# The last group of a latent-attention layer, its steps behind the attention in two halves of rows

## The chip, the cores and the metric

The kernel runs on one core of one Trainium2 chip. The core's engines are TensorE (PE in the views; PEld is its weight load), VectorE (DVE), ScalarE (ACT), GpSimd (POOL) and SyncE (SP, here only issuing DMAs). The metric is device time of one execution in microseconds (us); lower is better.

## The reference, cut to what matters

A two-layer pre-norm decoder on 4096 rows (16 sequences of 256) of width 256, all float32. The change touches only how the second layer's two attention parts end:

```python
x = x + _L1_attn_ref(_layernorm(x), ...)        # latent attention, 8 heads, latent rank 64
x = x + _L1_xattn_ref(_layernorm(x), ctx, ...)  # one head over 77 context rows, masked, bias
x = x + _L1_ffn_ref(_layernorm(x), ...)         # quantised feed-forward, 256 -> 768 -> 256

def _L1_ffn_ref(x, w_gate, w_up, w_down):
    def act_qdq(x):
        scale = max(max(abs(x)) / (2**15 - 1), 1e-12)   # one scale for the whole tensor
        return clip(round(x / scale), ...) * scale
    x = act_qdq(x)
    ...
```

The scale of `act_qdq` needs the largest magnitude over all 4096 normalised rows. So the feed-forward can't begin before the last row has gone through both attention parts and the last layer norm.

## The kernel before, in words

The program is written by hand, engine by engine, with semaphores; each engine runs its own list in order. Stages follow each other in blocks: layer 0, experts, `layer1` (latent attention and context attention, L1408 on), `feed_forward`. Each block ends with a barrier of all engines.

`layer1` works on eight groups of 512 rows (two sequences; four tiles of 128 rows, `NT` = 4, `NG` = 8). The attention itself runs in slots: `t` counts them, eight to a group (`NS` = 8: two sequences times four pairs of heads), so group `g` has slots 8g to 8g+7. In slot `t` TensorE does `scores(t)`, then `turn(t - 1)` (transposes of the probabilities), then `values(t - 2)`. DVE does the maxima, `by_key` (copies one half of the turned probabilities) and `invert`; ACT does `exponents(t)`, `heads(t - 2)` (copy of the head outputs) and its own `by_key(t - 1)`; POOL divides the probabilities by their sum. Around these stand, at fixed places of a slot, the other steps of the groups, with a group's tail running one to three groups late:

- `project(g, b)` (L1849): output projection of half `b` (256 rows) of a group, then `add_heads(g, b)` on DVE into `x4`.
- `moments(1, g)` (DVE: four BN_STATS, four BN_AGGR, the variance), `deviation` (POOL: a power of -0.5, L1725), `shifts` (DVE), `normalise` (ACT, four tiles, L1983), `turn_norm` (PE, eight transposes, L1825) and two copies of the banks to `hT` (ACT, L1949).
- `x_scores` (PE, L1866), `masked` (DVE, three operations, L2107 to L2114), `x_exponents` (ACT, L1988), `x_turn` (PE, L1874), a copy to `xPT` (ACT), `x_values` (PE, L1883, one bank for each 256 rows), `add_context` (DVE, L2127) into `x5`.
- `moments(2, g)`, `deviation`, `shifts`, `normalise`, `turn_norm`, the copies into `hT_all`, and `largest` (DVE, L2133) into `amax_all`. SyncE stores `x5` to DRAM.

For the last group (number 7, slots 56 to 63) nothing of a later group is left to run beside this tail. The loops run to slot `LAST` with the same placing: its `project(7, 1)` comes in slot 66, `turn_norm(1, 7)` in slot 69, and so on. Group 6's `x_turn`, `x_values`, `add_context`, `moments(2)` to `turn_norm(2)` lie in slots 64 to 68, between group 7's.

PSUM banks 5, 6 and 7 serve all these steps in turn: the table `UNITS` gives the order in which steps take a bank, and a step waits (`room`) until the contents of the step three places before it in that order have been read out.

```python
        for t in range(FIRST, LAST):
            g, s = group_step(t)
            for name, ahead, n in UNITS[s]:
                if there(g + ahead):
                    k = turn_of % 3
```

`feed_forward` begins with the largest magnitude: a transpose (L2317), a maximum, a spread (L2322), scale and its inverse, then the first 512 rows are quantised (L2465, L2467) and the matmuls with the gate weights start (L2309), without a gap from there on. Its last pass is the projection down (L2354).

## Time and profile before

| what | us |
| --- | --- |
| median of 3 runs (1717.52 to 1718.95) | 1718.71 |
| the profiled execution's own time | 1720.9 |
| its span, first to last instruction | 1719.2 |
| PE busy in the span | 1539.6 (90%) |
| DVE busy | 976.8 (57%) |
| ACT busy | 847.2 (49%) |
| POOL busy | 465.5 (27%) |
| last slot of attention starts (scores of slot 63 on PE) | 1348.78 |
| last copy of `layer1` ends (ACT) | 1396.55 |
| first gate matmul of `feed_forward` | 1402.10 |
| first matmul of the projection down | 1630.92 |

A busy share is an average over all stages. In the stretch that the change touches, PE is busy 13.94 of 24.50 us and every other engine less. In the chain and the timelines below, a time is us from the span's start; a wait stands in brackets behind an instruction, with the one that ended it. "x16" counts records: a float32 matmul leaves two, a transpose one.

### The profile page before, as it was taken

Reading aid. Unit: us, or ns where it says so; the run is one execution under the profiler, and the core shown is the slowest. Engines: PE = TensorE matmul, PEld = TensorE weight load, DVE = VectorE, ACT = ScalarE, POOL = GpSimd, SP = SyncE. Lnnn points to the kernel's source line nnn. Section 1 sums busy time; section 2 is a strip of 40 time slices with the busy share of each in tenths; the row PEclk is TensorE's granted clock in tenths of the full one; section 3 lists DMA queues with packets and bytes.
Section 4 is the critical chain, followed back from the end, with each engine's and each line's share of the span. In section 5 each row is a group of like instructions: output and inputs, shape, how many; then the busy total and the mean of one; then the engine's idle time right before and its main releaser. Section 6 shows DMA issues by size and latency. Waiting matters only on the chain. (4 is left out here: it accounts for less than half of the span.)

```text
span 1719.2 us, 26943 instructions
## 1 busy us (share of the span) xinstructions
PE 1539.6 (90%) x10059; PEld 1073.2 (62%) x10059; DVE 976.8 (57%) x2262; ACT 847.2 (49%) x1849; POOL 465.5 (27%) x582
## 2 busy tenths in 40 slices
PE   6999999998987889999998999999999869995099
PEld 4677776766665667777787566666666534442088
DVE  3665767766756335222222567667665535599883
ACT  4455564654465322211211565666665523596980
POOL 3222233243334310000002565554533200042000
PEclk9999999998999989999998999999999969998599
DMA  3440111111151143433425211101100000000022
GB/s 112 153 152 16 46 29 44 31 43 42 44 150 41 56 139 123 148 116 117 157 81 139 62 38 50 47 29 31 32 14 13 13 13 0 1 0 13 25 88 72
DMA packets 100912, 108.30 MB, mean 63 GB/s; under 512 B 25394, under 2 KB 89788, under 8 KB 100784
## 3 DMA queue, kind: packets, MB, share of 16 engines
q1 hardware_dynamic: 94640, 90.01, 16.7%
q0 software_dynamic: 6144, 16.57, 3.0%
q8 instruction: 82, 1.34, 0.3%
q14 instruction: 46, 0.38, 0.1%
HBM read 64.77 MB, written 42.01 MB: 62 GB/s over the span
## 5 line engine op out<-in xcount | busy, mean ns | idle before, releaser
L1740 POOL TENSOR_SCALAR c_pr<-c_pr,c_rsum 128x256 f32<-128x256 f32 x256 | 127.5, 515 | 189.4 <-DVE c_rsum L2046 188.7
L1961 ACT ACTIVATE c_pr<-bank,c_nmax 128x256 f32<-128x256 f32 x256 | 118.0, 473 | 119.2 <-DVE c_nmax L2041 111.8
L1511 ACT ACTIVATE b_G<-bank 128x320 f32<-128x320 f32 x128 | 56.0, 437 | 210.2 <-PE bank L1461 210.2
L1461 PE MATMUL bank<-b_XT,shared 128*128 128x320 f32 x512 | 154.0, 435 | 0.0
L2041 DVE TENSOR_REDUCE c_nmax<-bank 128x2 f32<-128x512 f32 x128 | 82.4, 685 | 106.0 <-PE bank L1791 102.9
L1475 PE MATMUL bank<-shared,b_G 128*128 128x256 f32 x640 | 142.2, 379 | 0.0
L1475 PEld LDWEIGHTS bank<-shared,b_G 128*128 128x128 f32 x640 | 120.9, 190 | 17.8
L1060 DVE TENSOR_TENSOR hT_all<-bank,a_causal 128x512 f32<-128x512 f32 x128 | 79.4, 682 | 65.9 <-PE bank L557 65.9
L492 POOL TENSOR_TENSOR a_L<-a_L,a_Lm 128x1232 f32<-128x1232 f32 x32 | 72.0, 2249 | 164.6 <-DVE a_Lm L1075 164.6
L1461 PEld LDWEIGHTS bank<-b_XT,shared 128*128 128x128 f32 x512 | 92.1, 192 | 27.3 <-issue 0.8
L1530 DVE COPY b_Y<-bank 128x256 f32<-128x256 f32 x80 | 33.9, 424 | 120.3 <-PE bank L1475 120.1
L1522 DVE COPY b_XT<-bank 128x256 f32<-128x256 f32 x80 | 34.0, 424 | 100.2 <-PE bank L1448 100.2
L2354 PE MATMUL bank<-wdT,d_raw 128*128 128x256 f32 x384 | 85.0, 385 | 2.5 <-DVE d_raw L2566 2.5
L2309 PE MATMUL bank<-hT_all,wgT 128*128 128x512 f32 x192 | 84.6, 604 | 2.0 <-DVE hT_all L2467 2.0
L1708 POOL MEMSET c_minus<- 128x4 f32 x1 | 0.1, 102 | 312.3 <-POOLq L54 312.3
L1802 PE MATMUL bank<-ident,c_pr 128*128 128x128 f32 x512 | 72.3, 281 | 12.2 <-POOL c_pr L1740 9.0
L2309 PE MATMUL bank<-hT_all,wuT 128*128 128x512 f32 x192 | 82.9, 593 | 0.0
L2354 PEld LDWEIGHTS bank<-wdT,d_raw 128*128 128x128 f32 x384 | 74.3, 194 | 12.9 <-DVE d_raw L2566 2.5
L1072 DVE TENSOR_TENSOR a_L<-bank,a_amask 128x308 f32<-128x308 f32 x128 | 52.2, 470 | 47.3 <-PE bank L572 30.2
L1802 PEld LDWEIGHTS bank<-ident,c_pr 128*128 128x128 f32 x512 | 55.0, 141 | 37.4 <-POOL c_pr L1740 24.7
L1791 PE MATMUL bank<-c_latT,c_qT 64*128 64x256 f32 x512 | 76.8, 407 | 0.6 <-ACT c_pr L1961 0.2
L507 POOL DMA_INDIRECT t_slots_in<-a_h,a_slot_s x64 | 63.2, 987 | 33.1 <-issue 17.1
(346 smaller groups left out, 3399.8 us busy)
## 6 DMA issues: line engine op xcount, KB each, us to landing
shared<-L_ffn_w SPq DMA_DIRECT2D x32, 512.0 KB, 6.0
t_slots_in<-a_h SPq DMA_DIRECT2D x20, 512.0 KB, 6.9
shared<-t_slots_in SPq DMA_DIRECT2D x15, 640.0 KB, 7.2
t_slots_out<-b_Y SPq DMA_DIRECT2D x15, 640.0 KB, 4.1
hT_all<-x SPq DMA_DIRECT2D x8, 512.0 KB, 4.1
a_xr<-x SPq DMA_DIRECT2D x8, 512.0 KB, 3.8
t_x_a<-a_x SPq DMA_DIRECT2D x8, 512.0 KB, 2.8
shared<-t_x_a SPq DMA_DIRECT2D x8, 512.0 KB
```

The costliest lines, as they stand in the source:

```text
L492: p.tensor_tensor(L[n % 2][:, :, :], L[n % 2][:, :, :], bcast(Lm[n % 2][:, :], 2, S2), ALU.subtract).then_inc(q.sub_ready, 1)
L507: p.indirect_dma_start(out=dr["slots_in"], out_offset=bass.IndirectOffsetOnAxis(ap=slot_s[:, k, j:j + 1], axis=0), in_=h2[i % 2][:, j, :], ...
L1060: v.tensor_tensor(A[:, rg, :, :, :].rearrange("p e k t -> p (e k) t"), P[rg][:, :].rearrange("p (n t) -> p n t", t=128), bcast(causal[:, : ...
L1461: t = p.matmul(P[2 + n % 2][:, 0:HC], w1[e % 3][:, u, 128 * f:128 * f + 128], XT[e % 2][:, u, HC * m:HC * m + HC], start=(u == 0), stop=(u ...
L1475: t = p.matmul(P[4 + n % 3][:, 0:D], G[e % 2][:, f, 128 * j:128 * j + 128], w2[e % 3][:, f, :], start=(f == 0), stop=(f == 3))
L1740: p.tensor_scalar(pr[k][:, e, u, :], pr[k][:, e, u, :], rsum[k][:, e, u:u + 1], 1.0, ALU.mult, ALU.mult).then_inc(q.pr_ready, 1)
L1791: x = p.matmul(P[e][:, S * u:S * u + S], qT[g % 2][r, m, S * b + 128 * u:S * b + 128 * u + 128], latT[g % 2][r, S * b:S * b + S], start=Tr ...
L1802: x = p.transpose(P[2 + e][:, S * k + 128 * u:S * k + 128 * u + 128], pr[t % 2][:, e, u, 128 * k:128 * k + 128], ident)
L1961: a.activation(pr[t % 2][:, e, u, :], P[e][:, S * u:S * u + S], ACT.Exp, bias=nmax[t % 2][:, e, u:u + 1], accum_out=sums[t % 2][:, e, u:u ...
L2041: v.tensor_reduce(nmax[t % 2][:, e, :], P[e][:, :].rearrange("p (u k) -> p u k", u=2), AX.X, ALU.max, negate=True).then_inc(q.nmax_ready, 1)
L2309: t = p.matmul(bank[:, :], wT[:, u, 128 * f:128 * f + 128], hT[:, u, T * g:T * g + T], start=(u == 0), stop=(u == 1))
L2354: t = p.matmul(P[n % 8][:, 0:D], raw[:, f, T * g + 128 * j:T * g + 128 * j + 128], wdT[:, f, :], start=(f == 0), stop=(f == FC - 1))
```

## The change

The loops of all engines end before slot 63 (`TAIL` = 63), and the rest, slot 63 and all that came after, is written out by hand:

- Slot 63 and what was slot 64 now have the attention's own steps first. On DVE, `by_key` and `invert` stand ahead of group 6's `masked`, and `penalties(7)` comes forward too. On PE, both last `values` stand ahead of group 6's `x_values`; the latter is cut in its two banks, the second behind `project(7, 1)`.
- Group 7's steps from the layer norm on work on half 0 and half 1 (256 rows, two tiles) apart: `moments`, `deviation`, `shifts`, `normalise`, `turn_half`, `x_scores_half`, `masked_half`, `x_exponents`, `x_turn_half`, `add_context_half`, and the same for the last norm and `largest`. Half 0 needs only `project(7, 0)`.
- A half's transposes for both 128-column parts go into one bank, read out by one copy. `TAIL_UNITS` gives the new order of banks.
- Group 7's result is added into `x4` in place, not into `x5`, and its last norm goes into `h[0]`, so that it doesn't wait for group 6's. SyncE stores it in two halves.
- Counted on all engines: DVE 16 rows of instructions more (1338 for 1322), ACT 4, PE 5, POOL 2, SP 1. Matmuls, exponentials and copies cover the same rows as before.

```diff
+        Z = NG - 1
+        TAIL = NS * Z + NS - 1
+        TAIL_UNITS = (("project0", Z, 1), ("xturn", Z - 1, 1), ("xout0", Z - 1, 2), ("project1", Z, 1), ("norm1_0", Z, 1), ("xout1", Z - 1, 2),
+                      ("xs_0", Z, 1), ("norm1_1", Z, 1), ("xturn_0", Z, 1), ("xs_1", Z, 1), ("xout0", Z, 2), ("xturn_1", Z, 1), ("xout1", Z, 2),
+                      ("turn2a", Z - 1, 1), ("turn2b", Z - 1, 1), ("norm2_0", Z, 1), ("norm2_1", Z, 1))
...
-                    if there(g - 2):
+                    if g - 2 == Z:
+                        for b in range(NB):
+                            wait_kept(s, f"xout{b}", Z)
+                            s.dma_start(x5_rows[Z][:, 2 * b:2 * b + 2, :], x4[Z % 2][:, 2 * b:2 * b + 2, :]).then_inc(q.stored, 16)
+                    elif there(g - 2):
...
-                for t in range(FIRST, LAST):
+                for t in range(FIRST, TAIL):
...
+                exponents(TAIL)
+                heads(TAIL - 2)
+                by_key(TAIL - 1)
+                x_exponents(Z - 1)
+                by_key(TAIL)
+                keep_unit("xturn", Z - 1, xPT[:, :], bank("xturn", Z - 1)[0:S2, :])
+                heads(TAIL - 1)
+                heads(TAIL)
+                normalise(1, Z, x4[Z % 2], 0)
+                keep_half("norm1_0", hT[:, :, 0:S])
+                normalise(1, Z, x4[Z % 2], 1)
+                x_exponents(Z, 0)
+                keep_half("norm1_1", hT[:, :, S:2 * S])
+                keep_x_turn(0)
+                x_exponents(Z, 1)
+                keep_x_turn(1)
+                normalise(2, Z - 1, x5)
+                normalise(2, Z, x4[Z % 2], 0)
+                keep_norm(2, Z - 1, [c.hT_all[:, u, T * (Z - 1):T * Z] for u in range(2)])
+                normalise(2, Z, x4[Z % 2], 1)
+                keep_half("norm2_0", c.hT_all[:, :, T * Z:T * Z + S])
+                keep_half("norm2_1", c.hT_all[:, :, T * Z + S:T * Z + T])
...
+                def turn_half(n, part, h_):
+                    name = f"norm{n}_{part}"
+                    room(p, name, Z)
+                    for j in rows_of(part):
+                        p.wait_ge(h_s[n], NT * Z + j + 1)
+                        for u in range(2):
+                            x = p.transpose(bank(name, Z)[:, S * u + 128 * (j % 2):S * u + 128 * (j % 2) + 128], h_[:, j, 128 * u:128 * u + 128], ident)
+                    x.then_inc(full(name, Z), 1)
```

What stands in a row on two engines, by lines and buffers (`bank5` is PSUM bank 5; `c_h_1` and `c_h_2` are the normalised rows of the first and the second norm, `c_h_0` an older room now used for the last norm of group 7; `x4_0` and `x5` belong to group 6, `x4_1` to group 7).

PE, from `project(7, 0)` on, before:

```order
L1856 MATMUL bank5<-c_wb,shared 128x256 x8
L1802 MATMUL bank2<-ident,c_pr_1 128x128 x4
L1802 MATMUL bank3<-ident,c_pr_1 128x128 x4
L1815 MATMUL bank4<-c_PT_0,c_lat_1 64x256 x4
L1874 MATMUL bank6<-ident,c_L 77x128 x4
L1883 MATMUL bank7<-hT_all,c_xPT 128x256 x2
L1883 MATMUL bank5<-hT_all,c_xPT 128x256 x2
L1815 MATMUL bank4<-c_PT_1,c_lat_1 64x256 x4
L1856 MATMUL bank6<-c_wb,shared 128x256 x8
L1825 MATMUL bank7<-ident,c_h_2 128x128 x4
L1825 MATMUL bank5<-ident,c_h_2 128x128 x4
L1825 MATMUL bank6<-ident,c_h_1 128x128 x4
```

The same place after:

```order
L1919 MATMUL bank5<-c_wb,shared 128x256 x8
L1838 MATMUL bank2<-ident,c_pr_1 128x128 x4
L1838 MATMUL bank3<-ident,c_pr_1 128x128 x4
L1937 MATMUL bank6<-ident,c_L 77x128 x4
L1851 MATMUL bank4<-c_PT_0,c_lat_1 64x256 x4
L1851 MATMUL bank4<-c_PT_1,c_lat_1 64x256 x4
L1948 MATMUL bank7<-hT_all,c_xPT 128x256 x2
L1919 MATMUL bank5<-c_wb,shared 128x256 x8
L1870 MATMUL bank6<-ident,c_h_1 128x128 x4
L1948 MATMUL bank7<-hT_all,c_xPT 128x256 x2
L1879 MATMUL bank5<-hT_all,c_hT 128x77 x4
L1870 MATMUL bank6<-ident,c_h_1 128x128 x4
```

Both `values` (L1815, now L1851) moved ahead of group 6's context values, of which the second bank now stands behind the transposes of half 0; half 0's context scores (L1879) stand ahead of the transposes of half 1.

DVE, from slot 63's copy to the end of group 6's additions, before:

```order
L2052 COPY c_PT_0<-bank3 128x512
L2046 RECIPROCAL c_rsum_1<-c_sums_1 128x4
L2091 TENSOR_TENSOR c_x4_1<-bank5,c_x3_1 128x512
L2052 COPY c_PT_1<-bank3 128x512
L2118 RECIPROCAL c_xr<-c_xsum 128x4
L2127 SCALAR_TENSOR_TENSOR c_x5<-bank7,c_xr,c_x4_0 128x256 x2
L2127 SCALAR_TENSOR_TENSOR c_x5<-bank5,c_xr,c_x4_0 128x256 x2
L2066 BN_STATS c_stats_2<-c_x5 128x6 x4
L2071 BN_AGGR c_mean_var_2<-c_stats_2 128x2 x4
L2073 TENSOR_SCALAR c_var_eps_2<-c_mean_var_2 128x4
L2091 TENSOR_TENSOR c_x4_1<-bank6,c_x3_1 128x512
```

The same place after, from `invert(63)`:

```order
L2166 RECIPROCAL c_rsum_1<-c_sums_1 128x4
L2229 TENSOR_TENSOR c_L<-bank7,c_keep 128x308
L2234 TENSOR_TENSOR c_L<-c_L,c_pen2 128x308
L2236 TENSOR_REDUCE c_xmax<-c_L 128x4
L2222 TENSOR_TENSOR c_pen2<-hT_all,c_keep 128x154 x2
L2225 TENSOR_TENSOR c_pen2<-c_pen2,c_pen 128x308
L2172 COPY c_PT_1<-bank3 128x512
L2213 TENSOR_TENSOR c_x4_1<-bank5,c_x3_1 128x512
L2187 BN_STATS c_stats_1<-c_x4_1 128x6 x2
L2192 BN_AGGR c_mean_var_1<-c_stats_1 128x2 x2
L2194 TENSOR_SCALAR c_var_eps_1<-c_mean_var_1 128x2
L2199 SCALAR_TENSOR_TENSOR c_shift_1<-c_mean_var_1,c_rstd_1 128x2
```

`masked(6)` and `penalties(7)` now stand behind `invert`, and half 0's moments and shift ahead of group 6's context addition.

DVE, the end of the block before:

```order
L2114 TENSOR_REDUCE c_xmax<-c_L 128x4
L2118 RECIPROCAL c_xr<-c_xsum 128x4
L2127 SCALAR_TENSOR_TENSOR c_x5<-bank7,c_xr,c_x4_1 128x256 x2
L2127 SCALAR_TENSOR_TENSOR c_x5<-bank5,c_xr,c_x4_1 128x256 x2
L2066 BN_STATS c_stats_2<-c_x5 128x6 x4
L2071 BN_AGGR c_mean_var_2<-c_stats_2 128x2 x4
L2073 TENSOR_SCALAR c_var_eps_2<-c_mean_var_2 128x4
L2077 SCALAR_TENSOR_TENSOR c_shift_2<-c_mean_var_2,c_rstd_2 128x4
L2133 TENSOR_REDUCE c_amax<-c_h_2 128x1
L2135 TENSOR_TENSOR amax_all<-amax_all,c_amax 128x1
```

The end after:

```order
L2199 SCALAR_TENSOR_TENSOR c_shift_2<-c_mean_var_2,c_rstd_2 128x2
L2253 RECIPROCAL c_xr<-c_xsum 128x2
L2257 SCALAR_TENSOR_TENSOR c_x4_1<-bank5,c_xr,c_x4_1 128x256 x2
L2187 BN_STATS c_stats_2<-c_x4_1 128x6 x2
L2192 BN_AGGR c_mean_var_2<-c_stats_2 128x2 x2
L2194 TENSOR_SCALAR c_var_eps_2<-c_mean_var_2 128x2
L2281 TENSOR_REDUCE c_amax<-c_h_2 128x1
L2284 TENSOR_TENSOR amax_all<-amax_all,c_amax 128x1
L2199 SCALAR_TENSOR_TENSOR c_shift_2<-c_mean_var_2,c_rstd_2 128x2
L2281 TENSOR_REDUCE c_amax<-c_h_0 128x1
L2284 TENSOR_TENSOR amax_all<-amax_all,c_amax 128x1
```

Half 1's context addition and moments (L2257, L2187) stand behind half 0's shift; group 6's largest magnitude stands between half 1's moments and its shift.

## Rows read from the trace of the kernel before

**Rows 1.** The chain that ended last, in order of time: start us, us, what.

```profile
1398.75 0.39 PE bank L2317
...
1402.10 88.08 PE bank L2309 x200
...
1630.92 85.06 PE bank L2354 x384
```

**Rows 2.** Timeline of PE: start us, us, engine line op out<-in xcount.

```profile
1299.14 1.98 PE L1866 MATMUL bank<-hT_all,c_hT 128*128 128x77 f32 x16
...
1353.15 3.72 PE L1856 MATMUL bank<-c_wb,shared 128*128 128x256 f32 x16
1356.71 1.04 PE L1802 MATMUL bank<-ident,c_pr 128*128 128x128 f32 x8
1357.68 1.08 PE L1815 MATMUL bank<-c_PT,c_lat 128*64 128x256 f32 x8
1360.04 1.99 PE L1883 MATMUL bank<-hT_all,c_xPT 77*128 77x256 f32 x8 [0.68 <-ACT c_xPT L1949]
...
1363.53 3.72 PE L1856 MATMUL bank<-c_wb,shared 128*128 128x256 f32 x16 [0.48 <-ACT shared L1968]
...
1375.73 3.67 PE L1866 MATMUL bank<-hT_all,c_hT 128*128 128x77 f32 x16 [0.73 <-issue]
1382.50 1.14 PE L1874 MATMUL bank<-ident,c_L 128*77 128x128 f32 x4 [3.10 <-ACT c_L L1988]
1384.32 3.78 PE L1883 MATMUL bank<-hT_all,c_xPT 77*128 77x256 f32 x8 [0.68 <-ACT c_xPT L1949]
```

**Rows 3.** Timeline of DVE, 1367 to 1389 us.

```profile
1367.29 0.69 DVE L2091 TENSOR_TENSOR c_x<-bank,c_x 128x512 f32<-128x512 f32 x1 [2.19 <-PE bank L1856]
...
1368.08 1.41 DVE L2066 BATCH_NORM_STATS2 c_stats<-c_x 128x6 f32<-128x256 f32 x4
...
1372.27 1.21 DVE L2133 TENSOR_REDUCE c_amax<-c_h 128x1 f32<-128x1024 f32 x1
...
1379.43 0.48 DVE L2107 TENSOR_TENSOR c_L<-bank,c_keep 128x308 f32<-128x308 f32 x1 [5.75 <-PE bank L1866]
...
1386.54 0.88 DVE L2127 SCALAR_TENSOR_TENSOR c_x<-bank,c_xr,c_x 128x256 f32<-128x256 f32 x2 [3.88 <-PE bank L1883]
1388.14 0.87 DVE L2127 SCALAR_TENSOR_TENSOR c_x<-bank,c_xr,c_x 128x256 f32<-128x256 f32 x2 [0.72 <-PE bank L1883]
```

**Rows 4.** Timeline of ACT, the last attention slot, the last copies and the last norm.

```profile
1353.36 0.21 ACT L1961 ACTIVATION_READ_ACCUMULATOR c_pr<-bank,c_nmax 128x1 f32 x1
...
1380.97 0.36 ACT L1988 ACTIVATE c_L<-c_L,c_xmax 128x77 f32<-128x77 f32 x1 [5.34 <-DVE c_xmax L2114]
...
1392.45 2.08 ACT L1983 ACTIVATE c_h<-c_x,c_shift,c_rstd 128x256 f32<-128x256 f32 x4 [8.19 <-DVE c_shift L2077]
1395.95 0.60 ACT L1949 ACTIVATE hT_all<-bank 128x512 f32<-128x512 f32 x1 [0.26 <-PE bank L1825]
```

**Rows 5.** Timeline of POOL, the power for group 7's last norm.

```profile
1391.21 1.01 POOL L1725 TENSOR_TENSOR c_rstd<-c_var_eps,c_minus 128x4 f32<-128x4 f32 x1 [20.02 <-DVE c_var_eps L2073]
```

**Rows 6.** Groups by line and form, 1371.6 to 1397 us: busy us, mean ns of one.

```profile
L2100 DVE TENSOR_TENSOR c_pen<-hT_all,c_keep 128x154 f32<-128x154 f32 x2 | 0.5, 310 | 0.0
L2103 DVE TENSOR_TENSOR c_pen<-c_pen 128x308 f32<-128x308 f32 x1 | 0.5, 479 | 0.0
```

**Rows 7.** Stretches: us; busy PE, PEld, DVE, ACT, POOL (count); PEclk; DMA share; GB/s.

```profile
1372.10:1396.60 24.50, 13.94 (x44) 9.72 (x44) 8.40 (x23) 8.05 (x21) 1.01 (x1) 0.50 0.06 21
1402.10:1405.90 3.80, 3.80 (x5) 1.73 (x6) 1.36 (x2) 0.00 (x0) 0.00 (x0) 0.50 0.00 0
1631.00:1634.60 3.60, 3.60 (x9) 2.88 (x10) 1.86 (x3) 3.60 (x4) 0.00 (x0) 0.50 0.00 0
935.90:941.80 5.90, 5.90 (x23) 5.90 (x24) 1.63 (x5) 1.34 (x4) 4.60 (x5) 0.50 0.36 99
1389.50:1392.00 2.50, 0.00 (x0) 0.00 (x0) 1.57 (x9) 0.00 (x0) 0.79 (x1) 0.50 0.61 210
```

More of the change, by code:

```diff
@@ L1660, in layer1, with rows_of, slice_of, turn_no @@
                 if there(g + ahead):
-                    k = turn_of % 3
-                    place[name, g + ahead] = (k, used[k], filled[k])
-                    used[k] += 1
-                    filled[k] += n
+                    give(name, g + ahead, n)
                     turn_of += 1
+        for name, i, n in TAIL_UNITS:
+            give(name, i, n)
+            turn_of += 1
         after = {name: n for units in UNITS.values() for name, _, n in units}
+        after.update({name: n for name, _, n in TAIL_UNITS})
+        def rows_of(part):
+            return range(NT) if part is None else range(2 * part, 2 * part + 2)
+        def slice_of(part):
+            return slice(0, NT) if part is None else slice(2 * part, 2 * part + 2)
+        def turn_no(i, part):
+            return i + 1 + (part or 0)
+        def rows_done(i, part):
+            return NT * i + (NT if part is None else 2 * part + 2)
         def bank(name, i):
@@ L1826, in turn_norm, with x_scores_half, x_turn_half @@
                         x.then_inc(full(name, i), 1)
+                def turn_half(n, part, h_):
[6 more added lines that the diff above has]
+                    x.then_inc(full(name, Z), 1)
+                def x_scores_half(part):
+                    wait_kept(p, f"norm1_{part}", Z)
+                    name = f"xs_{part}"
+                    room(p, name, Z)
+                    for j in rows_of(part):
+                        for u in range(2):
+                            x = p.matmul(bank(name, Z)[:, S2 * (j % 2):S2 * (j % 2) + S2], hT[:, u, 128 * j:128 * j + 128], xm[Z][:, u, part, :],
+                                         start=(u == 0), stop=(u == 1))
+                    x.then_inc(full(name, Z), 1)
+                def x_turn_half(part):
+                    name = f"xturn_{part}"
+                    p.wait_ge(q.xe_ready, rows_done(Z, part))
+                    room(p, name, Z)
+                    for j in rows_of(part):
+                        x = p.transpose(bank(name, Z)[0:S2, 128 * (j % 2):128 * (j % 2) + 128], L[:, j, :], ident)
+                    x.then_inc(full(name, Z), 1)
                 def latent(i):
@@ L1885, in x_values @@
                     x.then_inc(full(name, i), 1)
-                for t in range(FIRST, LAST):
+                for t in range(FIRST, TAIL):
                     g, s = group_step(t)
@@ L1924, in _ @@
                         project(g, 0)
+                scores(TAIL)
+                turn(TAIL - 1)
+                values(TAIL - 2)
+                project(Z, 0)
+                turn(TAIL)
+                x_turn(Z - 1)
+                values(TAIL - 1)
+                values(TAIL)
+                x_values(Z - 1, 0)
+                project(Z, 1)
+                turn_half(1, 0, h[1])
+                x_values(Z - 1, 1)
+                x_scores_half(0)
+                turn_half(1, 1, h[1])
+                x_turn_half(0)
+                x_scores_half(1)
+                x_values(Z, 0)
+                x_turn_half(1)
+                x_values(Z, 1)
+                turn_norm(2, Z - 1)
+                turn_half(2, 0, h[0])
+                turn_half(2, 1, h[0])
             @block.scalar
@@ L2021, in _, with keep_half, keep_x_turn @@
                         x_exponents(g - 1)
+                def keep_half(name, out):
+                    keep_unit(name, Z, out, bank(name, Z)[:, :].rearrange("p (u t) -> p u t", u=2))
+                def keep_x_turn(part):
+                    keep_unit(f"xturn_{part}", Z, xPT[:, S * part:S * part + S], bank(f"xturn_{part}", Z)[0:S2, 0:S])
+                exponents(TAIL)
[20 more added lines that the diff above has]
+                keep_half("norm2_1", c.hT_all[:, :, T * Z + S:T * Z + T])
             @block.vector
```

156 lines of the change are left out of this document (117 added, 39 removed).

## Prediction

> **What bounds the kernel now.** The chain of waits comes first. It starts at 1398.75 us, with the transpose that begins the feed-forward, and is gapless from there but for short issue times: the gate pass from 1402.10 us and the projection down from 1630.92 us are single pieces of TensorE work [rows 1]. Ahead of 1398.75 stands a barrier of all engines, at which the chain of the view breaks off. So what ends last in `layer1` moves everything behind it: no transfer and no other work is due at a fixed time in the feed-forward. That last thing is ACT's copy of the last bank, 1395.95 to 1396.55 us [rows 4]. From it to the first gate matmul are 5.55 us (barrier, scale, first quantisation), which the change doesn't touch.
>
> Next the timelines, backwards from that copy. There each engine waits for another one after the next: the last norm waited 8.19 us for DVE's shift [rows 4], DVE's addition 3.88 us for the context values [rows 3], the mask 5.75 us for the context scores [rows 3], the exponentials 5.34 us for the mask [rows 4], POOL's power 20.02 us for the variance [rows 5]. Between 1372.1 and 1396.6 us PE is busy 13.94 of 24.5 us, DVE 8.40, ACT 8.05 [rows 7]: one group's tail run in series, with nobody to fill the gaps. It begins where `project(7, 1)` starts, at 1363.53 us [rows 2], and takes 33.0 us to 1396.55. TensorE's granted clock is 0.50 in all of the last 24.5 us [rows 7], the lower of its two levels (1.2 GHz), after matmuls with pauses between them; its steps take nearly twice as long there: context scores 3.67 us against 1.98, context values 3.78 against 1.99 [rows 2].
>
> **The change, in the order of time.** Nothing before slot 63 moves. I follow each engine's new list with durations from the rows, and give the difference at four points of the chain.
>
> Point 1, the start of `project(7, 1)`. `project(7, 0)` at 1353.15 stays, and so does the transpose behind it at 1356.71 [rows 2]: `invert` comes earlier, but PE was busy until then. Behind it now come `x_turn(6)` (0.5), `values(62)` (1.0, its pitch being 1358.69 less 1357.68), a copy of the heads on ACT with its handoff (0.5) that `values(63)` waits for, `values(63)` (1.0) and one bank of context values (0.95, half of 1.99) [rows 2]: 1356.71 + 1.0 + 0.5 + 1.0 + 0.5 + 1.0 + 0.95 = 1361.7. Before: 1363.53. **1.8 us earlier.** What DVE's new order delays is hidden: behind the last exponential at 1353.55 [rows 4] come `invert` (0.15) and `masked(6)` (three operations of 0.48 [rows 3]), to 1355.2, then four exponentials (0.37 each, with one read of the accumulator behind the last) to 1356.75, and PE wants them at 1357.7: 0.95 us of cover.
>
> Point 2, the context scores of the last rows. The projection of half 1 is read out by 1366.15 (1361.7 + 3.75 + 0.7 [rows 2, 3]). By then half 0 has had its layer norm (its moments start at 1359.2, it is normalised by 1362.3, while PE projects), and PE turns it right behind the projection and scores it by 1367.8. On DVE, half 1's moments end at 1367.4: half of 1.41 plus half of the aggregates plus the variance, with 0.1 for handoffs, 1.25 in all [rows 3]. But its shift stands behind group 6's second context addition (0.85 [rows 3]) and half 0's mask. So it ends at 1369.3, and POOL's power is covered. Norm, transposes and copy of two tiles bring half 1's scores to 1371.75. Before, all scores began at 1375.73 [rows 2]. **4.0 us earlier in all.**
>
> Point 3, the end of the last context addition, before at 1389.0 (1388.14 + 0.87 [rows 3]), 13.3 us behind the start of the scores. Now: scores of two tiles 1.7 (between 1.0 and 1.87, the clock falling about then), mask 0.9, exponentials 0.85, transposes 0.7 with the wait for PE, which is then at half 0's context values, copy 0.4, context values 2.2, addition 0.9, handoffs: 1378.65 for the values. The shift of half 0's last norm stands ahead of the addition on DVE: half 0's values end at 1375.5, its addition at 1376.4, moments 1377.7, power 1378.3, shift 1378.55. Both waits end within 0.15 us of each other; the addition ends at 1379.55. **9.45 us earlier in all.**
>
> The half power has no row. Bounds: 1.01 us, what four columns take [rows 5], and half of that; a price under half would have to be a cost that falls faster than the columns. I take 0.56, nearer to proportion; at 1.01 the end is 0.45 later, since the shift waits longer.
>
> Point 4, the last copy. Moments of half 1 end at 1380.8. Then comes group 6's largest magnitude (1.21 [rows 3] and 0.2 for the maximum behind it), which covers half 1's power but holds its shift until 1382.4. Before, the norm behind that shift began at 1392.45 [rows 4]: 10.0 earlier. Then normalise, transpose and copy half as many rows: 2.4 us instead of 4.1 (ACT norm 2.08 for four tiles [rows 4], so 1.05; the second tile is turned 0.75 behind its start, and one copy of 0.6 instead of two in a row). End at 1384.8. **11.75 us earlier.** DVE's last magnitude ends at 1384.45, under it. The store of the last rows can go at 1379.6; before, a whole one could go at 1389.0 and its bytes fell into 1389.5 to 1392 [rows 7], so it is hidden, with 2 us to spare.
>
> In short: 1.8 from the order of the last attention slots, 2.2 from half 0's norm and mask beside the projection, 5.45 from the context part and 2.3 from the last norm in halves.
>
> **Small pieces.** A mask operation on 154 elements takes 310 ns in its group, one on 308 takes 479 [rows 6]: a half costs two thirds of a whole. The 0.9 above for three of them is this price. The Trainium skill (VectorE: DVE Perf Modes, "The TRN2 errata — SBUF-src ops pay a fixed extra latency per instruction") speaks against cutting: the latency is paid once for each tile, and it advises tiles of 512 elements and more. The trace agrees with its direction, 310 ns being more than half of 479. If the fixed part were everything, both masks would cost 1.5; that case is rival B.
>
> **The clock behind the block.** The gate pass starts at a granted 0.50 and stays there to 1405.9; the projection down does the same from 1630.9 to 1634.6: 3.8 and 3.7 us [rows 7]. Each us at that level costs 0.5 us of matmuls that have no gap. Another start in this trace stayed low for 5.9 us of gapless matmuls, from 935.9 to 941.8 [rows 7]. Both starts move in time, and before they are near the short end. From 3.75 to 5.9 for both would cost 2.15 us; I take 0.5, and keep 0 less 0.8 (the shorter that I can't exclude) to 2.15 for the range.
>
> **The sum.** 11.75 - 0.5 = 11.25 us. The profiled execution took 1720.9, so 1709.65; the median of the three runs is 2.2 lower, and with it 1718.71 - 11.25 = 1707.5 us.
>
> **The rivals.**
>
> A. The clock stays high in the tail. PE now has fewer pauses up to 1368 us. For it: with group 6's and group 7's steps mixed, pauses are shorter. Against: half 1's transposes and half 0's turn leave PE idle for over half of 1368 to 1371.7, as it was before the fall at 1372. At full clock scores take 1.0 and values 1.15 for each half, and the end comes at 1382.95, 13.6 earlier: 1718.7 - 13.6 = 1705.1, or 1704.6 with an early return of the clock.
>
> B. Pieces and handoffs cost more than rows say: masks as dear as whole ones (+1.2), the power at 1.01 (+0.45), and the clock's return at the long end (+1.6 more than I took): 1707.5 + 3.2 = 1710.7.
>
> C. The halves don't overlap, the change not doing what it says: if some wait of half 1 for half 0's room makes one whole chain after another, only the 1.8 us of point 1 are left: 1716.9. Against: the table of banks lets half 1's transposes wait only for half 0's copy (1366.5), and half 1's scores for the first mask operation.
>
> D. Slower. The sparser matmuls of the tail hold the clock low, and it does not come back in the gate pass. Each us at the low level there costs 0.5, so it eats the gain from 23.5 us on, and gives slower by over 0.2% from 30 us. If the whole gate pass to 1490 stays low it is 1707.5 + 42 = 1749. Against: it returned within 5.9 us in each of the three places [rows 7].
>
> **Chances.** Forecast (1706 to 1709.5) 0.62, A 0.13, B 0.17, C 0.04, D 0.03, and 0.01 for something that I don't see. The range is 1704.6 (A with an early clock) to 1710.7 (B). Under 0.2%, 3.4 us, a measurement of this kernel can't tell a change from none; faster is below 1715.3. A, B and the forecast are all faster: 0.93. C is the same: 0.04. Slower: 0.03.
>
> **What would show it.** In the changed kernel's timelines: `project(7, 1)` at 1361.7; half 1's context scores at 1371.7; the last context addition's end at 1379.6; the last copy's end at 1384.8; the first gate matmul 5.55 behind it. A power on two columns of 0.56. The clock falling near 1372, and low for 3.7 to 6 us in the gate pass and in the projection down. Wrong is: an end of the block beyond 1387 or before 1382; DVE busy where I have it waiting for PE (then its order is the bound, not the chain); a difference behind 1405 that isn't the clock's.

## The result, and the profile after

| what | before | after |
| --- | --- | --- |
| median of 5 runs, us | 1718.95 (1717.52 to 1720.25) | 1709.57 (1709.1 to 1711.8) |
| the profiled execution's own time | 1720.9 | 1711.8 |
| its span | 1719.2 | 1710.1 |
| `project(7, 0)` starts | 1353.15 | 1353.43 |
| `project(7, 1)` starts | 1363.53 | 1362.04 |
| context scores of the last rows start | 1375.73 | 1371.98 |
| last context addition ends | 1389.01 | 1381.51 |
| last copy of `layer1` ends | 1396.55 | 1386.67 |
| first gate matmul | 1402.10 | 1393.43 |

The changed kernel takes 0.9939 of the time of the one before, 95% interval 0.9924 to 0.9954: 9.4 us less of the medians, 9.1 us less of the two profiled executions. It is faster, and inside the range, but 2.1 us of the forecast gain of 11.25 are missing. Counted one by one, DVE has 2272 instructions for 2262, ACT 1850 for 1849, POOL 584 for 582, and PE 10059 in both.

The chain of waits of after has the two pieces of [rows 1] again, 8.67 and 8.94 us earlier:

```profile
1393.43 87.79 PE bank L2492 x200
...
1621.98 84.91 PE bank L2537 x384
```

PE's timeline of after answers to [rows 2]. The columns are as there: start, duration, engine, line, operation, and the wait before it in brackets.

```profile
1353.43 3.72 PE L1919 MATMUL bank<-c_wb,shared 128*128 128x256 f32 x16
...
1361.07 1.13 PE L1948 MATMUL bank<-hT_all,c_xPT 77*128 77x256 f32 x4
1362.04 3.62 PE L1919 MATMUL bank<-c_wb,shared 128*128 128x256 f32 x16
...
1366.80 1.10 PE L1879 MATMUL bank<-hT_all,c_hT 128*128 128x77 f32 x8
1370.21 1.09 PE L1870 MATMUL bank<-ident,c_h 128*128 128x128 f32 x4 [2.31 <-ACT c_h L2074]
...
1371.98 1.99 PE L1879 MATMUL bank<-hT_all,c_hT 128*128 128x77 f32 x8
...
1377.08 2.08 PE L1948 MATMUL bank<-hT_all,c_xPT 77*128 77x256 f32 x4 [0.47 <-ACT c_xPT L2036]
...
1390.08 0.37 PE L2500 MATMUL bank<-ident,amax_all 128*1 128x128 f32 x1 [4.05 <-PEq L54]
```

Up to half 1's context scores (L1879 at 1371.98) the order of work stands as it was forecast, within 0.35 us. The last line is the first instruction behind the block. Its wait is for the barrier (L54), not for data.

DVE's timeline of after, from half 0's context addition on, answers to [rows 3]:

```profile
1375.87 0.88 DVE L2257 SCALAR_TENSOR_TENSOR c_x<-bank,c_xr,c_x 128x256 f32<-128x256 f32 x2 [0.77 <-PE bank L1948]
...
1376.78 0.75 DVE L2187 BATCH_NORM_STATS2 c_stats<-c_x 128x6 f32<-128x256 f32 x2
1379.10 0.25 DVE L2192 BATCH_NORM_AGGREGATE c_mean_var<-c_stats 128x2 f32<-128x6 f32 x2 [1.56 <-ACT c_h L2074]
...
1380.36 0.16 DVE L2199 SCALAR_TENSOR_TENSOR c_shift<-c_mean_var,c_rstd 128x2 f32<-128x2 f32 x1 [0.81 <-POOL c_rstd L1756]
...
1380.63 0.88 DVE L2257 SCALAR_TENSOR_TENSOR c_x<-bank,c_xr,c_x 128x256 f32<-128x256 f32 x2
```

Between the statistics and the aggregates DVE stands still for 1.56 us, waiting for ACT. What ACT does then, and its last copy (timeline of ACT, as [rows 4]):

```profile
1376.93 2.06 ACT L2074 ACTIVATE c_h<-c_x,c_shift,c_rstd 128x256 f32<-128x256 f32 x4
...
1386.07 0.60 ACT L2036 ACTIVATE hT_all<-bank 128x512 f32<-128x512 f32 x1 [0.29 <-PE bank L1870]
```

POOL's last power (timeline of POOL, as [rows 5]):

```profile
1382.86 0.70 POOL L1756 TENSOR_TENSOR c_rstd<-c_var_eps,c_minus 128x2 f32<-128x2 f32 x1 [2.54 <-DVE c_var_eps L2194]
```

Each engine ends its list of a block with a DRAIN, an instruction of its queue that isn't counted as busy time, and then meets the others at the barrier. The drains of `layer1` stand on the line that opens the block: engine, instruction, count, duration in ns (least/median/greatest), start. After:

```profile
L1719 POOLq DRAIN  x1: 6039/6039/6039, 1382.8 to 1382.8; - x1
...
L1719 ACTq DRAIN  x1: 626/626/626, 1386.1 to 1386.1; - x1
```

Before:

```profile
L1693 POOLq DRAIN  x1: 6349/6349/6349, 1391.2 to 1391.2; - x1
...
L1693 ACTq DRAIN  x1: 626/626/626, 1396.0 to 1396.0; - x1
```

POOL's drain starts with its last power and goes on for 5.3 us behind it: to 1388.85 after, to 1397.55 before. ACT's ended at 1386.7 and 1396.6. In both kernels the barrier waited for POOL, and the first gate matmul came 4.55 to 4.58 us behind the end of that drain. The last power ended at 1392.22 before [rows 5] and ends at 1383.56 after: 8.66 us earlier, which is what the gate matmul gained, 8.67. Where the last copy stood didn't decide.

### The profile page after: what moved, and what is told of

Same layout as the page of the kernel before. It is cut to its first block and busy times, and to the rows that moved or that the text cites. A ratio compares the mean times of both kernels' runs of the same rounds, so it can differ in the third digit from the quotient of the medians.

```text
span 1710.1 us, 26964 instructions
## 1 busy us (share of the span) xinstructions
PE 1536.0 (90%) x10059; PEld 1071.3 (63%) x10059; DVE 980.1 (57%) x2272; ACT 848.6 (50%) x1850; POOL 467.3 (27%) x584
## 5 line engine op out<-in xcount | busy, mean ns | idle before, releaser
L684 PE MATMUL bank<-ident,a_L 128*77 128x128 f32 x512 | 67.2, 285 | 6.9 <-ACT a_L L932 3.2
```

The lines of the kernel that those rows point to most:

```text
L684: x = p.transpose(bank(name, i)[0:S2, 128 * k:128 * k + 128], L[n % 2][:, 4 * rg + k, :], ident)
```

## The experiments

The kernel before alone has medians from 1704.73 to 1720.29 us in the sessions of these runs, and on one and the same chip 1705.17 in one session and 1720.29 in another. So times are compared only with those of before, or of after, taken in the same session on the same chip: x1 to x4, x5 and x6, x7 to x10, and x11 and x12 are the four sessions. Since a total moves by some us with the clock in stages that no experiment touches, most verdicts rest on one distance in the trace: from the start of `project(7, 0)` to the first gate matmul. It is 48.95 us before (1353.15 to 1402.10) and 40.00 after (1353.43 to 1393.43).

| kernel | distance | forecast | ratio to before, with interval |
| --- | --- | --- | --- |
| x10: after again | 40.02 | 40.0 | 0.9939 (0.9922 to 0.9957) |
| x1: group 6's norm earlier | 38.64 | 38.6 | 0.9949 (0.9932 to 0.9966) |
| x2: POOL's last work late | 41.90 | 41.8 | one run |
| x5: halves, old order | 41.16 | 41.0 | 0.9962 (0.9949 to 0.9975) |
| x6: new order, whole | 47.00 | 47.1 | 0.9985 (0.9969 to 1.0000) |
| x4: matmuls as filler | 38.64 | see there | 0.9944 (0.9921 to 0.9967) |
| x7: drain early | 37.84 | 37.8 | 0.9936 (0.9917 to 0.9955) |
| x8: x1, x4 and x7 together | 35.09 | 35.2 | 0.9926 (0.9909 to 0.9943) |
| x12: x1 and x7 together | 36.46 | 36.5 | 0.9934 (0.9914 to 0.9954) |

The intervals of x1, x4, x7, x8 and x12 all hold after's 0.9939: that they differ from after is shown by the distance in one trace each, not by time. The distance is good to about 0.25 us. It is 40.00, 40.02, 39.99 and 40.02 in after, x10, x3 and x11, which have the same instructions there, but 39.75 in x9, which has them too: there the clock fell 18.4 us behind the start of `project(7, 0)` instead of 16.0 to 16.4, and half 1's scores start 18.33 us behind it instead of 18.55.

**The two parts apart.** x5 takes the halves with the order that slots 63 and 64 had before (lists of PE and DVE; the table of banks and ACT's list follow, and on DVE group 6's two context additions stand together ahead of `add_heads(7, 1)`):

```diff
                 turn(TAIL)
-                x_turn(Z - 1)
                 values(TAIL - 1)
-                values(TAIL)
+                x_turn(Z - 1)
                 x_values(Z - 1, 0)
+                x_values(Z - 1, 1)
+                values(TAIL)
                 project(Z, 1)
-                x_values(Z - 1, 1)
...
+                masked(Z - 1)
                 invert(TAIL)
-                masked(Z - 1)
                 penalties(Z)
-                by_key(TAIL)
                 add_heads(Z, 0)
+                by_key(TAIL)
```

> The halves stay, the order of slots 63 and 64 goes back: group 6's mask ahead of slot 63's copy and inverse, group 6's context values (both banks) ahead of the last values of the attention. Theory by my sum: project(7, 1) starts 1.8 us later (1363.8 against 1362.0), but group 6's second context addition is then out of the way of half 1's shift, so that half 1's context scores start only about 1.0 us later (1373.0 against 1372.0), and the gate pass too. Rival (the order is worth all of its 1.8 us, or nothing because the clock and DVE take it back): 1.8 or 0.

x6 is the kernel before with the new order of the last slots, group 7's steps whole (PE's list; the other engines' follow it):

```diff
+                scores(TAIL)
+                turn(TAIL - 1)
+                values(TAIL - 2)
+                project(Z, 0)
+                turn(TAIL)
+                x_turn(Z - 1)
+                values(TAIL - 1)
+                values(TAIL)
+                x_values(Z - 1, 0)
+                project(Z, 1)
+                x_values(Z - 1, 1)
+                turn_norm(1, Z)
+                x_scores(Z)
+                turn_norm(2, Z - 1)
+                x_turn(Z)
```

> The order of slots 63 and 64 as changed, but no halves: group 7's norms, scores, mask, values in whole groups, group 6's last norm in ACT's idle time. Theory by my sum: project(7, 1) at 1362.0, the context scores at 1374.1 (before 1375.7), the last addition ends at 1387.4, the first gate matmul at 1400.5: 1.6 us earlier than before and 7.1 later than with halves. Rival (most of the gain is order and overlap with group 6, not the halves): first gate matmul before 1397.

From PE's timeline of x5 (both projections, half 1's scores):

```profile
1342.70 3.72 PE L1919 MATMUL bank<-c_wb,shared 128*128 128x256 f32 x16
1353.07 3.72 PE L1919 MATMUL bank<-c_wb,shared 128*128 128x256 f32 x16 [0.48 <-ACT shared L2055]
...
1362.51 1.90 PE L1879 MATMUL bank<-hT_all,c_hT 128*128 128x77 f32 x8
```

From that of x6 (both projections, the whole scores):

```profile
1334.45 3.72 PE L1872 MATMUL bank<-c_wb,shared 128*128 128x256 f32 x16
1343.05 3.62 PE L1872 MATMUL bank<-c_wb,shared 128*128 128x256 f32 x16
...
1355.04 3.67 PE L1882 MATMUL bank<-hT_all,c_hT 128*128 128x77 f32 x16 [0.73 <-issue]
```

`project(7, 1)` starts 10.37 us behind `project(7, 0)` in x5, as before the change (10.38 [rows 2]), and 8.60 in x6, as after (8.61): the order is worth 1.8 us there, as forecast. At the gate matmul the order alone has given 1.95 us (48.95 to 47.00) and the halves alone 7.79 (48.95 to 41.16). Together they give 8.95, so 0.8 us of the two overlap: with halves, the scores of half 1 stand only 1.26 us earlier for the new order (19.81 against 18.55 behind `project(7, 0)`). The halves do overlap, and rival C falls: x5 and x6 each have one part, and the halves are 78% of the gain (7.00 of 8.95, from x6 to after) to 87% (7.79, alone).

**The wait that was missed.** In after, group 6's last norm stands behind half 1's exponentials on ACT, and its shift behind half 1's mask on DVE. x1 moves both ahead:

```diff
+                normalise(2, Z - 1, x5)
                 x_exponents(Z, 1)
                 keep_x_turn(1)
-                normalise(2, Z - 1, x5)
...
+                shifts(2, Z - 1)
                 masked_half(1)
                 add_context_half(0)
-                shifts(2, Z - 1)
```

> Group 6's last shift and norm are moved ahead of half 1's mask and exponentials, so that DVE's aggregates for half 0's last norm no longer wait 1.56 us for ACT. Theory (that wait is the step I missed): the aggregates start at about 1377.6 instead of 1379.1, the last context addition at 1379.2 instead of 1380.6, POOL's last power and the first gate matmul are 1.4 us earlier (1392.0 against 1393.4). Rival (the context values on PE are as late as DVE): DVE's wait goes to the values of half 1, which end at 1379.2, and the gain is under 0.3 us.

DVE's timeline of x1, the aggregates of both halves of the last norm, and between them half 1's context addition:

```profile
1358.69 0.25 DVE L2192 BATCH_NORM_AGGREGATE c_mean_var<-c_stats 128x2 f32<-128x6 f32 x2
...
1360.38 0.88 DVE L2257 SCALAR_TENSOR_TENSOR c_x<-bank,c_xr,c_x 128x256 f32<-128x256 f32 x2 [0.19 <-PE bank L1948]
...
1362.08 0.25 DVE L2192 BATCH_NORM_AGGREGATE c_mean_var<-c_stats 128x2 f32<-128x6 f32 x2
```

ACT's timeline of x1, the last copy:

```profile
1365.82 0.60 ACT L2036 ACTIVATE hT_all<-bank 128x512 f32<-128x512 f32 x1 [0.30 <-PE bank L1870]
```

POOL's drain in x1:

```profile
L1719 POOLq DRAIN  x1: 6037/6037/6037, 1362.6 to 1362.6; - x1
```

The bracket behind the aggregates is gone, and the gate matmul comes 1.36 us earlier. The other 0.2 of the 1.56 us are taken by what waits next: half 1's addition now waits 0.19 us for the context values on PE, so the expectation's rival is right for that part. The distance from the last copy's end (1366.42) to the gate matmul (1373.18) is 6.76 us, as in after: this moved copy and power alike, so it doesn't tell yet which of them the barrier waits for.

**What the barrier waits for.** x2 lets POOL wait for the last normalised tile, with one small fill behind it (a constant over itself). The last copy stays where it is; POOL's last work moves from 1383.5 to what would be 1385.4 in after's time.

```diff
                 deviation(2, Z, 1)
+                p.wait_ge(h_s[2], NT * NG)
+                p.memset(minus[:, 0:1], -0.5).then_inc(q.c_pool, 1)
```

> One memset of 128x1 is added on POOL, waiting for the last normalised tile (1385.3). Theory (the block's end waits for POOL's drain, 5.3 us behind POOL's last instruction of whatever kind): POOL's drain ends at about 1390.7 instead of 1388.9 and the first gate matmul is 1.8 us later. Rival a (the 5.3 us belong to the power instruction): drain ends at 1388.9 as before, no change. Rival b (the barrier waits for the store or for PE): no change either, with the drain's end away from the barrier.

POOL's drain in x2:

```profile
L1719 POOLq DRAIN  x1: 5422/5422/5422, 1368.5 to 1368.5; - x1
```

ACT's last copy in x2:

```profile
1369.21 0.60 ACT L2038 ACTIVATE hT_all<-bank 128x512 f32<-128x512 f32 x1 [0.30 <-PE bank L1872]
```

ACT's last copy starts 32.64 us behind `project(7, 0)`, as in after (1386.07 less 1353.43), and the gate matmul comes 1.90 us later. POOL's drain is again 5.3 us longer than the work that it closes, and the gate matmul 4.55 us behind its end (1373.92 to 1378.47). So POOL's drain, which begins with POOL's last instruction, sets the end of the block, not ACT's copy.

x7 puts a drain where POOL has nothing to do for long, behind the power of half 0's first norm:

```diff
                 deviation(1, Z, 0)
+                p.drain()
```

> One drain instruction is added on POOL behind the power of half 0's first norm, where POOL has 6.3 us without work; nothing else changes. In the changed kernel the first gate matmul starts 40.0 us behind the start of project(7, 0). Theory a (the 5.3 us are paid once, at the first drain behind the block's gathers): the new drain takes 5.3 us under other engines' work, the one at the block's end under 1 us, the barrier then waits for ACT's last copy, and the distance is 37.8: 2.2 us less. Theory b (every drain of POOL in a block with gathers takes 5.3 us): the last one ends where it did, 40.0. A drain longer than 6.3 us would hold the next power and make it more.

The early drain in x7:

```profile
L1780 POOLq DRAIN  x1: 6047/6047/6047, 1358.7 to 1358.7; - x1
```

The drain at the block's end in x7:

```profile
L1719 POOLq DRAIN  x1: 799/799/799, 1380.9 to 1380.9; - x1
```

ACT's last copy in x7, and the first gate matmul (chain of waits):

```profile
1384.11 0.60 ACT L2037 ACTIVATE hT_all<-bank 128x512 f32<-128x512 f32 x1 [0.30 <-PE bank L1871]
```

```profile
1389.30 89.08 PE bank L2493 x200
```

The price is paid once: the second drain ends 0.1 us behind the last power. The gate matmul comes 2.16 us earlier, now 4.59 us behind the end of the last copy (1384.71 to 1389.30), which decides at last. On this chip x7 took 1706.87 us (4 runs), after (x10) 1708.53 (6 runs).

> The changed kernel itself on this chip, beside the kernel before, for the ratio and the landmarks: 40.0 us from project(7, 0) to the first gate matmul, ratio 0.994 as before.

x10 is after once more, and its distance repeats to 0.02 us.

**What POOL's drain is a price of.** Not the power: x3 puts one power on a single column behind POOL's last work of the feed-forward, whose block ends with such a drain too.

```diff
+                p.memset(probe[:, 0:1], 2.0).then_inc(q.probed, 1)
+                p.memset(probe[:, 1:2], -0.5).then_inc(q.probed, 1)
+                p.wait_ge(q.probed, 2)
+                p.tensor_tensor(probe[:, 2:3], probe[:, 0:1], probe[:, 1:2], ALU.pow).then_inc(q.probed, 1)
```

> One power on 128x1 and two small memsets are added on POOL at the end of its work in the feed-forward, where the block has no gathers. Before, POOL's drain there took 1.15 us with a scaling in it. If the power makes the drain long, the drain there takes over 5 us now; if the gathers (indirect DMAs) of the block do, it stays under 2 us. No change of time: POOL has 140 us to spare there.

x9 puts one gather by row numbers there (an indirect DMA, which POOL issues and then waits for), x11 eight of them in a row:

```diff
+                p.memset(probe[:, 0:1], 0).then_inc(q.probed, 1)
+                p.wait_ge(q.probed, 1)
+                for n in range(8):
+                    p.indirect_dma_start(out=probe_x[:, 0:2], out_offset=None, in_=dr["wt"].rearrange("g p (a n) -> (g p a) n", n=2),
+                                         in_offset=bass.IndirectOffsetOnAxis(ap=probe[:, 0:1], axis=0),
+                                         bounds_check=127, oob_is_err=False).then_inc(q.probed_dma, 16)
+                    p.wait_ge(q.probed_dma, 16 * n + 16)
```

> One gather (indirect DMA of 8 bytes a partition) and a memset are added on POOL at the end of its work in the feed-forward, where POOL's drain took 1.15 us without them and 0.67 us with a power in front. If a gather in the block is what makes POOL's drain long, the drain there takes 5 us or more; if not (length or kind of the block's other work does), it stays under 2 us. No change of time.

> After with eight gathers on POOL, one behind the other, at the end of the feed-forward (useless work; nothing is left out). The drain at a block's end took 5.3 us on POOL in the blocks with 64 gathers, 0.67 us at the end of the feed-forward without one and 0.13 us there behind a single one. If what POOL pays is a price for each gather, 5.3 / 64 = 0.083 us, the drain at the end of the feed-forward takes about 0.7 us (0.03 + 8 x 0.083). If it depends on something else that the attention blocks do on POOL (the divisions of the probabilities, say), it stays below 0.3 us. If a few gathers in a row are enough for the whole price, it is near 5 us. What lies ahead is the same as in after: 40.0 us from the first projection of the last group to the first gate matmul, and 3.4 to 6 us at the low clock at the start of the gate pass.

The power and the drain at the end of the feed-forward in x3:

```profile
1550.61 0.56 POOL L2490 TENSOR_TENSOR d_probe<-d_probe 128x1 f32<-128x1 f32 x1
```


```profile
L2463 POOLq DRAIN  x1: 671/671/671, 1550.6 to 1550.6; - x1
```

The same in x9, behind one gather:

```profile
L2464 POOLq DRAIN  x1: 129/129/129, 1572.6 to 1572.6; - x1
```

The same in x11, behind eight:

```profile
L2464 POOLq DRAIN  x1: 701/701/701, 1599.5 to 1599.5; - x1
```

In x3 the drain starts with the power and is hardly longer than it, so a power leaves about 0.1 us behind. The 0.67 us that the expectation of x11 names for none is this one, mostly the power. In x9 and x11 POOL has waited for its transfers when the drain starts (x11's last gather ends at 1597.08), so the time is the drain's own: 0.13 us behind one gather, 0.70 behind eight, 0.082 for each more. By its own words the expectation of x9 had put 0.13 us down as a sign against the gathers (5 us or more, or not they); only x11 shows that the price goes by their number. `layer1` has 64 gathers, and 64 times 0.082 is 5.2 us, where 5.3 are seen. Two blocks of the kernel before fit as well. The end of layer 0, which also has 64 indirect DMAs (the last one ended 1.5 us ahead of this drain):

```profile
L369 POOLq DRAIN  x1: 5288/5288/5288, 616.4 to 616.4; - x1
```

The experts' block, which has none:

```profile
L1406 POOLq DRAIN  x1: 34/34/34, 622.5 to 622.5; - x1
```

The gathers are a cause that the numbers support at 0, 1, 8 and 64 of them. No run takes `layer1`'s own gathers away, so for its 5.3 us this is argued from the other blocks, and what POOL does in the drain no view shows. x7 says that it needn't wait for the end of the block.

**The clock.** x4 fills pauses of PE in the tail with seven matmuls of 512 columns whose results nobody reads: two each behind three steps and one ahead of the gate pass (two of the four places are shown).

```diff
+                def fill(n):
+                    for k in range(n):
+                        p.matmul(P[0][:, :], wb[:, 0, 0:128], wb[:, 0:2, :].rearrange("p m n -> p (m n)"), start=True, stop=True)
...
                 turn_half(2, 0, h[0])
+                fill(2)
                 turn_half(2, 1, h[0])
+                fill(2)
```

> Seven matmuls of 128x512 without use are added in TensorE's idle times: two ahead of half 1's transposes, two ahead of the last transposes, two behind them, one behind the spread of the scale. Theory (the granted clock follows PE's activity, and costs the tail and the start of the gate pass): the clock stays at 1.00 from 1350 us to 1397, context scores of a half take 1.1 instead of 2.0 us, values 1.1 instead of 2.0, and the gate pass starts at full clock: 1.7 us there and 1 to 2 us in the tail, 3 us in all. Rival (other engines set the tail, and the clock falls anyway, in the stretch of 1372 to 1382 that has no filler): no gain or, the fillers running at half speed, up to 1.5 us slower.

PE's timeline of x4 at the places of half 1's scores and half 0's and 1's context values:

```profile
1356.82 1.12 PE L1879 MATMUL bank<-hT_all,c_hT 128*128 128x77 f32 x8
1357.78 1.86 PE L1948 MATMUL bank<-hT_all,c_xPT 77*128 77x256 f32 x4
...
1361.05 2.08 PE L1948 MATMUL bank<-hT_all,c_xPT 77*128 77x256 f32 x4 [0.47 <-ACT c_xPT L2043]
```

Half 1's scores took 1.12 us instead of 1.99, and the distance fell by 1.36 us; the context values stayed long, 1.86 and 2.08, since the clock still fell at 1357.9. The gate pass took 86.71 us against 87.79. That makes 2.4 us of the 3 expected, in this trace; the ratio, 0.9944, doesn't show it. The clock didn't stay high, as the theory had it: it was low from 1357.9 to 1364.7 and again from 1375.0, 2.1 us ahead of the gate pass, to 1378.4.

x8 has the earlier norm, the early drain and six of the seven fillers; x12 has the first two alone, each with the edits shown above.

> Group 6's last norm early (x1), fillers on TensorE (x4, one matmul fewer at the end) and the early drain (x7) together. If theory a holds: the last copy ends at 30.7 us behind the start of project(7, 0), the first gate matmul at 35.2 instead of 40.0, and the gate pass starts at full clock, 1 us more: 5.8 us less than the changed kernel, 0.990 of the kernel before. If theory b holds: 37.3 and 3.7 us less in all.

> After with the two changes that saved time each by itself: group 6's last shift and norm ahead of half 1's mask and exponentials on DVE and ACT (1.36 us), and POOL's drain taken early, while POOL waits anyway (2.16 us); no useless matmuls. If the two add up, the distance from the start of project(7, 0) to the first gate matmul is 40.0 - 1.36 - 2.16 = 36.5 us (after: 40.0), and the time is 3.5 us less than that of after, within 1.5 us for the clock's return: ratio to before 0.9919, between 0.991 and 0.993. Rival: with the drain gone, something else ends late at the barrier (ACT's copy of the last bank ends later than POOL can), and what the earlier norm gave is already in it: 37.8 us, ratio 0.9925. Second rival: the clock, which falls in the tail in either case, returns later the earlier the gate pass starts; then the distance is 36.5 us, and less than 2 us of the 3.5 arrive.

Stretches of after at the start of the gate pass and of the projection down, as [rows 7] (stretch, us, busy PE, PEld, DVE, ACT, POOL, granted clock, DMA share, GB/s):

```profile
1393.40:1396.80 3.40, 3.37 (x4) 1.51 (x5) 1.39 (x2) 0.00 (x0) 0.00 (x0) 0.50 0.00 0
...
1621.98:1625.50 3.52, 3.52 (x8) 2.86 (x9) 1.86 (x3) 3.52 (x5) 0.00 (x0) 0.50 0.00 0
```

The start of the gate pass in x4:

```profile
1377.10:1378.40 1.30, 1.28 (x2) 0.77 (x3) 1.26 (x2) 0.00 (x0) 0.00 (x0) 0.50 0.00 0
```

In x7:

```profile
1389.30:1395.30 6.00, 6.00 (x7) 2.52 (x8) 2.05 (x3) 0.60 (x1) 0.00 (x0) 0.50 0.00 0
```

In x8, with the stretch ahead of it:

```profile
1379.00:1385.80 6.80, 4.89 (x18) 2.08 (x16) 3.88 (x12) 2.44 (x5) 0.70 (x1) 1.00 0.10 33
1387.30:1392.70 5.40, 5.37 (x7) 2.25 (x8) 2.08 (x3) 0.60 (x1) 0.00 (x0) 0.50 0.00 0
```

The longest and the shortest without fillers, in x5 and x6:

```profile
1383.86:1389.90 6.04, 6.04 (x7) 2.52 (x8) 2.05 (x3) 0.60 (x1) 0.00 (x0) 0.50 0.00 0
```

```profile
1381.45:1384.45 3.00, 3.00 (x4) 1.45 (x5) 1.36 (x2) 0.00 (x0) 0.00 (x0) 0.50 0.00 0
```

In x12:

```profile
1387.65:1391.60 3.95, 3.94 (x5) 1.85 (x6) 1.36 (x2) 0.13 (x1) 0.00 (x0) 0.50 0.00 0
```

Both combined kernels gave the distance to 0.1 us: x8 35.09, x12 36.46. So the earlier norm (1.36) and the early drain (2.16) add up, and neither hides the other: 40.00 less 3.52 is 36.48. In x8 the clock was at its full level in the last stretch of the tail and fell just ahead of the gate pass, where it stayed low for 5.4 us. The fillers gave 1.4 us in the distance (36.46 to 35.09). Whether they cost anything behind it isn't shown, since 5.4 lies inside what kernels without fillers have. The expectation of 5.8 us in all, with the gate pass at full clock, failed in its clock: the gain of 4.9 us in the distance is 2.3 us of the medians (1706.2 and 1708.53 on the same chip).

The other term is how long a start stays low. At the start of the gate pass it is 3.0 us in x6, 3.3 in x10, 3.4 in after, 3.5 in x11, 3.7 in x3, 3.9 in x12, 4.0 before, 4.9 in x2, 5.0 in x1, 5.4 in x8, 6.0 in x7 and x9 and 6.1 in x5. At half a us for each, that is 1.5 us of noise. Only x4 is outside, with 1.3, and there the clock had been low for 2.1 us when the pass began. The five traces with the same instructions (after, x3, x9, x10, x11) alone spread from 3.3 to 6.0. At the start of the projection down, behind work that no edit changed, the 14 traces have 3.1 to 6.0 us.

x12 or x7 should beat both kernels, and in the traces they do: x7's span is 1705.4 us where x10 has 1706.8 on the same chip, and x12's is 1704.2 where x11, which is after with hidden gathers, has 1707.1 on the same chip. By time the matter is not settled. x12 has 1706.65 us (6 runs, 1705.56 to 1711.32) and 0.9934 of before, and the interval of 0.9914 to 0.9954 holds after's 0.9939. Its expectation had the ratio between 0.991 and 0.993, which 0.9934 misses, though in its trace the distance is as forecast and the rest of the span behind the gate matmul is 316.6 us, against 316.7 in after and 315.8 in x10.

## Why the prediction came out as it did

The sign, the range and the place of the gain were right; the size was 11.25 us where 9.1 came in the profiled executions. The median, 1709.57, lies just above the forecast's own band (1706 to 1709.5), inside the range that rival B bounds. By its own steps:

- **Point 1**, `project(7, 1)` at 1361.7: 1362.04. `project(7, 0)` itself stands 0.28 later than before the change, so the step is right to 0.1 us, and x6 shows it alone.
- **Point 2**, half 1's scores at 1371.75: 1371.98. Right. The masks cost 0.31, 0.32 and 0.31 us for a half (L2242 to L2247 on DVE), as taken from [rows 6]. The Trainium skill (VectorE: DVE Perf Modes, "The TRN2 errata — SBUF-src ops pay a fixed extra latency per instruction") has the latency paid once for each tile. The trace agrees in direction again: the whole ones took 0.45 to 0.50.
- **Point 3**, the last addition's end at 1379.55: 1381.51, 1.96 late. This is the first step that failed. I wrote that half 0's moments end at 1377.7, from durations on DVE and values on PE, and left out what `moments` waits for. Before it writes `mean_var`, it waits until the norm that last read that buffer is through: group 6's, on ACT from 1376.93 to 1378.99. The wait of 1.56 us is in the trace, and x1 takes it away and gets 1.36 back. The change moved group 6's norm behind half 1's exponentials on ACT; I followed DVE's queue past the moved steps, but not ACT's for its reader. Of the other 0.4 us, 0.3 were there before the moments, as `project(7, 0)` started 0.28 later, and the power is 0.14: 0.70 us for two columns, not 0.56, inside its bounds.
- **Point 4**, 5.25 us from there to the last copy's end: 5.16. Right; the copy's end is late only by what point 3 left.
- **The fixed 5.55 us** to the gate matmul: 6.76, the second step that failed, and the largest single error beside the wait. It is no fixed piece. It was the 4.55 us behind the end of POOL's drain, and POOL's drain ended 1.0 us behind the last copy before. The halves shortened what follows the last power (norm, turn, copy) from 4.33 us (1392.22 to 1396.55) to 3.11 (1383.56 to 1386.67), but not the drain, which begins with the power. So 1.2 us of point 4's gain were never to be had. The drains stood in the trace of before; I took the barrier's length from the last copy, without asking which engine arrived last. By the prediction's own sign of being wrong (an end of the block beyond 1387) the copy, at 1386.67, stays inside, but the drain that ended the block, at 1388.85, doesn't.
- **The clock behind the block**: +0.5 taken, -0.43 measured (gate matmul to the end of the span: 317.10 before, 316.67 after). Inside the bounds, and in my favour by 0.9. The returns in the other runs spread over 3 us, so this was luck of one execution.
- **The store** is hidden, as said: SyncE waited 1.8 us for it and then 5.2 us more at the barrier.

In sum: 1.87 us late at the last copy and 1.21 at the barrier, less 0.93 for the clock, is 2.15, which is 11.25 less 9.1.

**The rivals.** A (clock high in the tail) didn't come: it fell at 1369.6 us, before half 1's scores, and x4 shows that it falls for 6.8 us even between seven extra matmuls. C falls by x5 and x6. D falls: the clock came back within 3.6 us in both passes. B's result is near to what was measured (1709.57 against 1710.7), but not by its prices: the masks cost what I took for them, the clock's return less than that, and only the power's 0.14 is of its kind. That the range held is in part luck: two waits that no rival named make up most of the 3.1 us by which the gate matmul came late, and what B had set aside for masks and clock covered them. The 0.93 for faster is the 0.92 of A, B and the forecast with the 0.01 for what I didn't see.

## What to carry to other kernels

When a step moves in a queue, follow also the steps that wait for its buffers to be free: here the last norm's statistics were on time and its aggregates stood behind another engine's older norm. And a gap at a barrier isn't a constant: find the engine that arrives last by the drains before and after, since shortening the others stops paying when that one decides. On an engine that has issued many gathers, a drain taken in a pause costs one line and takes its price off the end: 2.16 us of the distance here, too little for these times to show.

## What the runs showed of the hardware

- GpSimd's drain at the end of a block took 5.3 us of its own in each block with 64 indirect DMAs, and 0.03, 0.13 and 0.70 us with none, one and eight. In `layer1` of after the last gather had ended at 1221.4 us, 161 us ahead of the drain; in layer 0, 1.5 us ahead. It is paid once: behind an early drain the next one adds 0.1 us.
- A power on GpSimd took 1.01 us for four columns, 0.70 for two and 0.56 for one (128 partitions): about 0.4 us and 0.15 a column.
- TensorE's clock at the start of a gapless pass came back after 3.0 to 6.1 us in 13 of the 14 traces (1.3 in x4, where it was already low), and after 3.3 to 6.0 in the five with the same instructions; in x8 after 5.4 us even behind a stretch of 6.8 us at the full level that ended 1.5 us ahead of the pass.
